# A two-layer graph network: another node order and packet size in the second edge layer, another placing of the sort's matmuls in the first

## What is computed

```python
def reference(x, src, dst, edge_type_8, L0_gnn_weight, L0_gnn_bias, L1_gnn_W_self, L1_gnn_W_neigh):
    edge_index = jnp.stack([src, dst])
    h = jnp.maximum(_layernorm(x, axis=-1), 0.0)
    x = x + _L0_gnn_ref(h, edge_index, edge_type_8, L0_gnn_weight, L0_gnn_bias)
    h = jnp.maximum(_layernorm(x, axis=-1), 0.0)
    x = x + _L1_gnn_ref(h, L1_gnn_W_self, L1_gnn_W_neigh, src, dst)
    return x
# L0: row, col = edge_index (so row = src, col = dst)
#     out = segment_sum((h[col] @ weight[edge_type]), row);  relu(out + bias)
# L1: h_self = feat @ W_self;  h_neigh = feat @ W_neigh
#     h_sparse = h_neigh with all but the 32 largest of each row set to 0
#     h_self + segment_sum(h_sparse[src], dst) / max(degree(dst), 1)
```

## Time and profile before

| | us |
|---|---|
| median of 3 runs | 3860.12 (3858.58 to 3865.2) |
| profiled execution, its own time | 3839.47 |
| span of the profile | 3837.8 |
| VectorE busy | 3257.8 (85%) |
| TensorE busy | 2697.9 (70%) |
| GpSimd busy | 2214.7 (58%) |
| ScalarE busy | 1896.3 (49%) |

### The profile page before, as it was taken

The page is one execution under the profiler, slowest core; times in us unless marked ns, Lnnn a source line. Parts: engine busy times, 40 slices in busy tenths (PEclk is TensorE's granted clock), DMA queues, the critical chain, the costliest instruction groups (busy, mean ns, idle before and its releaser), DMA issues.

```text
span 3837.8 us, 66966 instructions
## 1 busy us (share of the span) xinstructions
PE 2697.9 (70%) x10746; PEld 1702.6 (44%) x10747; DVE 3257.8 (85%) x14074; ACT 1896.3 (49%) x5805; POOL 2214.7 (58%) x1536
## 2 busy tenths in 40 slices
PE   2554767667788888886777777777777755767776
PEld 1222655555566666665333333333333324445554
DVE  8998778888888888885799999999999994555556
ACT  0000233333333333333577767777677756777776
POOL 0001886667777777777455555555555535565554
PEclk9998888888899999998888888888888888888888
DMA  9600466666555555555244444444444427777776
GB/s 349 231 0 29 76 116 146 147 146 143 103 101 100 102 100 100 101 101 105 106 161 159 153 153 158 161 157 157 153 157 161 159 106 234 227 245 236 240 231 201
DMA packets 307277, 576.89 MB, mean 150 GB/s; under 512 B 32005, under 2 KB 187944, under 8 KB 307214
## 3 DMA queue, kind: packets, MB, share of 16 engines
q1 hardware_dynamic: 211598, 419.86, 32.6%
q0 software_dynamic: 95616, 156.31, 20.9%
HBM read 317.16 MB, written 258.88 MB: 150 GB/s over the span
## 4 chain that ended last, share of the span: by engine, by line
DVE 38%; issue 32%; PE 15%; DMA 5%; POOL 3%; DVEq 3%; ACT 2%; ACTq 0%; POOLq 0%; another core or an unknown queue 0%; SPq 0%
DVE zone_c L1148 12%; PE banks L1516 7%; DVE best L1143 6%; DMA agg<-msg,sidx 4%; PE banks L1418 3%; DVE zone_c L1155 3%; DVE zone_c L1032 2%; DVE zone_c L1036 2%; DVE zone_c L1034 2%; DVE cross L932 2%; PE banks L1361 2%; PE banks L1429 2%; POOL rows_in L647 1%; DVE zone_c L1182 1%; DVE stats L878 1%
## 5 line engine op out<-in xcount | busy, mean ns | idle before, releaser
L1494 PE MATMUL banks<-w,hT 128*128 128x512 f32 x1568 | 836.3, 695 | 192.3 <-ACT hT L1282 192.3
L659 POOL DMA_INDIRECT agg<-msg,sidx x400 | 658.0, 1645 | 223.2 <-issue 114.3
L647 POOL DMA_INDIRECT rows_in<-in_x,gidx x400 | 436.1, 1090 | 480.5 <-DVE gidx L894 350.1
L1148 DVE MATCH_REPLACE8 zone_c<-best,zone_c 128x256 f32<-128x256 f32 x1568 | 623.1, 407 | 0.0
L1182 DVE SCALAR_TENSOR_TENSOR zone_c<-banks,rdeg,zone_c 128x256 f32 x784 | 379.3, 484 | 287.0 <-PE banks L1516 151.5
L1516 PE MATMUL banks<-w,zone_c 128*128 x1568 | 460.8, 452 | 228.5 <-issue 88.3
L1494 PEld LDWEIGHTS banks<-w,hT 128*128 128x128 f32 x1568 | 340.1, 223 | 632.5 <-issue 522.0
L1143 DVE MAX8 best<-zone_c 128x8 f32<-128x256 f32 x1568 | 547.5, 410 | 4.2
L703 POOL TENSOR_TENSOR zone_c<-msg,zone_c 128x1024 f32<-128x1024 f32 x98 | 232.7, 2374 | 512.3 <-ACT zone_c L1270 512.3
L718 POOL DMA_INDIRECT w<-hs,gidx x392 | 371.3, 947 | 263.0 <-issue 121.3
L1418 PE MATMUL banks<-w,hT 128*128 x1600 | 480.3, 428 | 19.0 <-issue 17.4
(11 more groups left out here) (224 smaller groups left out, 5057.8 us busy)
## 6 DMA issues: line engine op xcount, KB each, us to landing
out_rows<-zone_c SPq DMA_DIRECT2D x196, 512.0 KB, 2.6
agg<-bias SPq DMA_DIRECT2D x2, 25344.0 KB, 102.9
zone_c<-agg SPq DMA_DIRECT2D x98, 512.0 KB, 4.7
hs<-zone_c SPq DMA_DIRECT2D x98, 512.0 KB, 3.0
zone_c<-out_rows SPq DMA_DIRECT2D x98, 512.0 KB
rows_in<-in_x SPq DMA_DIRECT2D x97, 512.0 KB, 3.9
keyrow<-key_rows SPq DMA_DIRECT2D x100, 320.0 KB
zone_c<-bucket_rows SPq DMA_DIRECT2D x25, 512.0 KB
```

What stands on the lines that cost most here:

```text
L647: pool.indirect_dma_start(out=rows_in[p][:, j, :], out_offset=None, in_=x[:, :], in_offset=bass.IndirectOffsetOnAxis(ap=gidx[p][:, j:j + 1 ...
L659: pool.indirect_dma_start(out=agg[:, :], out_offset=bass.IndirectOffsetOnAxis(ap=sidx[p][:, j:j + 1], axis=0), in_=msg[p][:, j * D:(j + 1) ...
L1148: last = v.match_replace(work[:, j, :], best[:, j, :], (work if k else neigh[p])[:, j, :], NEG)
L1494: last = mm(bank[4 + j][:, :], hT[p][:, c, j * P:(j + 1) * P], w1[:, c, :], start=(c == 0), stop=(c == KC - 1))
```

## The change

Three things change.

1. **Nodes per bucket.** The bucket of node n is no longer n / 128 but (n / 512) * 4 + n mod 4, and its place in the bucket is (n / 4) mod 128. So one partition's rows of a group of four buckets are four neighbouring rows of DRAM, and the loads and stores of `y` become 4 KB runs. `bucket_row`, `bucket`, `low7` and `low16` are computed in another way, with as many VectorE instructions as before. The type sort still needs the true target, so the first *sort* body gets four more VectorE instructions of 128x512 that encode the new number (`encode`).
2. **Ranking.** `RC` goes from 16 to 14 and `RCHUNKS` from 25 to 28, so *rank* has 30 bodies and *rest* 2. The pad for tiles beyond 392 is gone.
3. **TensorE's order.** `hist_count`, `rank_choose` and `sort_place` have their waits at j = 2 and their matmuls in two halves, behind j = 2 and j = 3.

```diff
-        RC, RCHUNKS = 16, 25
+        RC, RCHUNKS = 14, 28
...
-                sp.dma_start(y[:, g * B:(g + 1) * B, :], out[bass.ds(k * BE, BE), :].rearrange("(j p) d -> p j d", p=P)
+                sp.dma_start(y[:, g * B:(g + 1) * B, :], out[bass.ds(k * BE, BE), :].rearrange("(p j) d -> p j d", j=B)
...
-                sp.dma_start(out[bass.ds(k * BE, BE), :].rearrange("(j p) d -> p j d", p=P), y[:, q * B:(q + 1) * B, :]
+                sp.dma_start(out[bass.ds(k * BE, BE), :].rearrange("(p j) d -> p j d", j=B), y[:, q * B:(q + 1) * B, :]
...
-            link(v.tensor_scalar(tmp_i[:, :], from0[:, :], 7, None, ALU.arith_shift_right))
-            link(v.tensor_copy(bucket[:, :], tmp_i[:, :]))
-            link(v.tensor_scalar(code16_i, from0[:, :], P - 1, None, ALU.bitwise_and))
-            link(v.tensor_copy(low7[:, :], code16_i))
-            link(v.tensor_scalar(tmp_i[:, :], tmp_i[:, :], LO - 1, None, ALU.bitwise_and))
-            link(v.tensor_copy(low16[:, :], tmp_i[:, :]))
             link(v.tensor_scalar(tmp_i[:, :], from0[:, :], 9, None, ALU.arith_shift_right))
             link(v.tensor_copy(high16[:, :], tmp_i[:, :]))
+            link(v.tensor_scalar(code16_i, from0[:, :], LO - 1, None, ALU.bitwise_and))
+            link(v.tensor_copy(low16[:, :], code16_i))
+            link(v.scalar_tensor_tensor(bucket[:, :], tmp_i[:, :], float(LO), code16_i, ALU.mult, ALU.add))
+            link(v.tensor_scalar(tmp_i[:, :], from0[:, :], 2, None, ALU.arith_shift_right))
+            link(v.tensor_scalar(tmp_i[:, :], tmp_i[:, :], P - 1, None, ALU.bitwise_and))
+            link(v.tensor_copy(low7[:, :], tmp_i[:, :]))
...
                         slots_of_positions()
+                        link(v.scalar_tensor_tensor(tab["type"][:, :], bucket[:, :], float(P), low7[:, :], ALU.mult,
+                                                    ALU.add))
+                        encode(tab["type"][:, :], DST_CODE)
...
+            def half(j, n):
+
+                return range((2 * j - B) * n // B, (2 * j - B + 2) * n // B)
...
             def sort_place(c, p, j):
-                if j == 0:
+                if j == B // 2:
                     pe.wait_ge(sort_hot, c + 1)
-                for t in range(j * CC // B, (j + 1) * CC // B):
+                for t in half(j, CC):
...
-                    if phase == "sort":
+                    if j >= B // 2 and phase == "sort":
                         sort_place(c, pc, j)
```

More of the change, by code:

```diff
@@ L622, in _ @@
             nc.gpsimd.memset(raw["dst"][:, last, :], N).then_inc(consts, 1)
-            nc.gpsimd.memset(starts_pad[:, :, :], 0.0)
             nc.gpsimd.memset(ident[:, :], 0.0)
@@ L779, in _ @@
                 link(v.tensor_copy(rawf[n][:, :, :], raw[n][:, :, :]))
-            for shift_by, rows16 in ((7, bucket_row), (9, high_row)):
-                link(v.tensor_scalar(raw["type"][:, :, :], raw["dst"][:, :, :], shift_by, None, ALU.arith_shift_right))
-                link(v.tensor_copy(rows16[:, :, :], raw["type"][:, :, :]))
+            link(v.tensor_scalar(raw["type"][:, :, :], raw["dst"][:, :, :], 9, None, ALU.arith_shift_right))
+            link(v.tensor_copy(high_row[:, :, :], raw["type"][:, :, :]))
+            link(v.tensor_scalar(raw["dst"][:, :, :], raw["dst"][:, :, :], LO - 1, None, ALU.bitwise_and))
+            link(v.scalar_tensor_tensor(bucket_row[:, :, :], raw["type"][:, :, :], float(LO), raw["dst"][:, :, :],
+                                        ALU.mult, ALU.add))
             v.memset(key0[:, SLOTS:COLS], float(N)).then_inc(rawf_done, 1)
@@ L786, in _, with encode @@
                 link(v.tensor_copy(tab[n][:, :], bank[k][:, :]))
+            def encode(number, code):
+                link(v.tensor_scalar(tmp_f[:, :], number, float(HALF), float(SIGN - HALF), ALU.is_ge, ALU.mult))
+                link(v.scalar_tensor_tensor(code16[:, :], number, float(CODE), tmp_f[:, :], ALU.add, ALU.add))
+                link(v.tensor_copy(field(code), code16[:, :].bitcast(F16)))
             for n, code in (("src", SRC_CODE), ("dst", DST_CODE)):
[L789 to L791 removed]
+                encode(tab[n][:, :], code)
             link(v.tensor_copy(from0[:, :], tab["dst"][:, :]))
[L793 to L798 removed]
             link(v.tensor_scalar(tmp_i[:, :], from0[:, :], 9, None, ALU.arith_shift_right))
             link(v.tensor_copy(high16[:, :], tmp_i[:, :]))
+            link(v.tensor_scalar(code16_i, from0[:, :], LO - 1, None, ALU.bitwise_and))
[4 more added lines that the diff above has]
+            link(v.tensor_copy(low7[:, :], tmp_i[:, :]))
             for r in range(R):
@@ L1373, in edge0_degree @@
                     last.then_inc(degrees0, 1)
+            def half(j, n):
+                return range((2 * j - B) * n // B, (2 * j - B + 2) * n // B)
             def hist_count(c, p, j):
-                if j == 0:
+                if j == B // 2:
                     pe.wait_ge(hist_hot, c + 1)
                     wait_from(pe, hist_out, c - 1, c, 2)
-                for t in range(j * HC // B, (j + 1) * HC // B):
+                for t in half(j, HC):
                     last = mm(bank[SORT + p][0:HI, t * LO:(t + 1) * LO], high_hot[p][:, t, :], low_hot[p][:, t, :],
@@ L1385, in rank_choose @@
             def rank_choose(c, p, j):
-                if j == 0:
+                if j == B // 2:
                     pe.wait_ge(rank_hot, c + 1)
                     wait_from(pe, rank_own, 4 * (c - 1), c, 2)
-                for t in range(j * RC // B, (j + 1) * RC // B):
-                    if isinstance(c, int) and c * RC + t >= TILES:
-                        of = starts_pad[0:HI, c * RC + t - TILES, :]
-                    else:
-                        of = starts16[0:HI, bass.ds(c * RC + t, 1), :].rearrange("p t l -> p (t l)")
+                for t in half(j, RC):
+                    of = starts16[0:HI, bass.ds(c * RC + t, 1), :].rearrange("p t l -> p (t l)")
                     last = mm(bank[SORT + p][:, t * 2 * LO:(t + 1) * 2 * LO], high_of[p][0:HI, t * P:(t + 1) * P], of,
@@ L1449, in edge0_body @@
                     edge0_degree(b, p, j)
-                    if phase == "hist" and c < HCHUNKS:
+                    if j >= B // 2 and phase == "hist" and c < HCHUNKS:
                         hist_count(c, pc, j)
-                    if phase == "rank" and inside(c, RCHUNKS):
+                    if j >= B // 2 and phase == "rank" and inside(c, RCHUNKS):
                         rank_choose(c, pc, j)
-                    if phase == "sort":
+                    if j >= B // 2 and phase == "sort":
                         sort_place(c, pc, j)
```

4 lines of the change are left out of this document (removed).

## The result

| | before | after |
|---|---|---|
| median | 3864.13 us (3858.58 to 3868.43, 7 runs) | 3845.33 us (3840.57 to 3852.68, 7 runs) |
| ratio | | 0.9951, 95% interval 0.9937 to 0.9964 |
| span of the profile | 3837.8 us | 3843.6 us |

The account below looks back on a forecast made before the run. VectorE with TensorE's late product bound sort; near-equal engines and DMA latency the second edge layer. Terms 0.5 - 2 - 8.7 + 2.5 - 26 - 9 = -42.7 took 3860.1 to 3817.4 us, range 3783 to 3850.

Parts of the forecast that it names:

- Term 4: Second edge layer: 4 KB transfers of y cut 0.47 us from each of 37 landing waits; half counted, -9 us.
- Term 2: Ranking: 14 tiles a group give 28 bodies of 14.65 us and three fewer of rest, -8.7 us.
- Term 1: Sort: TensorE's wait for one-hots moves behind product 2, so VectorE waits less for std, -26 us.
- term 3: In hist, the same matmul reordering, but GpSimd is the bound there, -2 us.
- Rival A: Sort: the stall only moves as TensorE's clock falls, bodies stay at 13.64 us, total 3843 us; 15%.
- the break-even: Ranking: a body of 14.96 us, at which the smaller groups neither gain nor lose.
- Rival D: Ranking: bodies do not shrink, the adds' latency holds them at 15.3 us, total 3837 us; 15%.
- the small ones: Four new VectorE instructions in the first sort body, +2.5 us, and changed instructions in the preparation, +0.5 us.
- Rival B: The second edge layer follows its DMA time, so all 46 us go, total 3780 us; 12%.
- E: Second edge layer: transfers of y stay at 1 KB runs, no gain there, total 3826 us; 2%.
- Rival C: Second edge layer: long packets of y hold gathers longer, 76 us over 37 waits, total 3902 us; 8%.
- The sentence that the prediction would be wrong altogether: Sign: the prediction fails if the second edge layer moves by more than 30 us either way.

Follow-up runs that it names:

- rc14_only: Only the ranking group size changed, 14 tiles in place of 16, against the kernel before; ratio 0.9993.
- late_only: Only TensorE's new matmul order, against the kernel before; ratio 0.9911, median 3827.8 us.
- late_rc14: TensorE's new order and 14 tiles a group, without the new node numbers and 4 KB transfers, against the kernel before; ratio 0.993, median 3834.5 us.
- late_y: TensorE's new order with the new node numbers and 4 KB transfers, 16 tiles a group, against the kernel before; ratio 0.9898.
- late_y_2: TensorE's new order with the new node numbers and 4 KB transfers, ranking as before, against the kernel before on chip D; ratio 0.9913.
- after_2: The full changed kernel once more, against the kernel before on chip D; ratio 0.9924.
- late_only_2: Only TensorE's new matmul order, repeated against the kernel before on chip D; ratio 0.991.
- y_quarter: The kernel before with only one of four buckets of y loaded and stored per group, against the kernel before; ratio 0.9799.
- after_again: The full changed kernel, unchanged, run again against the kernel before on chip B; ratio 0.9949, median 3841.3 us.
- y_half_rows: The kernel before with only two of four buckets of y loaded and stored per group, against the kernel before; ratio 1.006.
- y_half_cols: The kernel before with only 128 of 256 columns of y loaded and stored, against the kernel before; ratio 1.0045.

## Why the prediction was wrong in size, point by point

Two steps of the sum failed. Term 4 took 0.47 us off each of 37 waits for a landing, 9 us after halving, and got nothing: the sum of the packet times fell, the time for which the transfers of `y` last did not. Term 2 took a ranking body of 14.65 us, 8.7 us in all, where bodies measured 14.82 to 14.96 and the part gave 4 us at best. A cost that stood in no term, some 7 us in *sort*, came on top. Term 1 (with term 3) gave some 6 us more than forecast, which was luck; without it the result would have been further off.

**Term 1, TensorE's order: right, a little low.** Forecast -26 us, and -28 with term 3, which the same edit brings; measured -34 (chip B) and -33 (chip D, 3773.9 against 3807.3). In the traces *sort* fell by 28.5 us on chip B (750.4 in rc14_only, 721.9 in late_only), with `std` waits of 19.7 us against the 19 worked out, and the body is 13.12 us where 13.1 was read off. That GpSimd holds it there was argued and is not tested. The 4 us allowed for the low clock were not needed: the granted clock fell from 0.96 to 0.95 and the bodies shrank all the same. Rival A is refuted.

**Term 2, ranking: the body of 14.65 us failed.** A body shrank to 14.82 (after) and 14.87 to 14.96 elsewhere; 14.96 is the break-even that the prediction itself names. VectorE's busy time per body fell by 333.0 / 25 - 355.86 / 28 = 0.61 us, and the body by 0.52 in the profile of after. I had taken 0.69, more than VectorE's own saving, because earlier products were to help GpSimd's adds. The adds do land in time more often (40.5 to 19.7 us of waits), but they don't with earlier products alone (37.7 us in late_only, whose body stays at 15.3 us), and VectorE's wait for gathers rose from 20.3 to 25.4 us, GpSimd's for `msg` from 20.0 to 32.6. So about -4 us in the profile of after in place of -8.7, -2.7 by the ratio of rc14_only with an interval that reaches past zero, and a loss of 3 to 7 us on top of the late matmuls. Rival D, bodies that don't shrink, is half right.

**A term that was not there: +7 us in *sort*.** With all three parts the sort body is 13.26 to 13.29 in each of three traces; with the late matmuls and one other part (late_rc14, late_y, late_y_2) it is 13.13 to 13.16. The costliest sort one-hots on VectorE, late_y_2 first and after_2 behind:

```profile
L1038 DVE TENSOR_SCALAR zone_c<-iota_h,fields 128x128 f16<-128x128 f16 x383 | 131.0, 342 | 2.0
L1042 DVE TENSOR_SCALAR zone_c<-iota_h,fields 128x392 f16<-128x392 f16 x384 | 123.0, 320 | 0.0
```

```profile
L1036 DVE TENSOR_SCALAR zone_c<-iota_h,fields 128x128 f16<-128x128 f16 x385 | 127.6, 332 | 2.0
L1040 DVE TENSOR_SCALAR zone_c<-iota_h,fields 128x392 f16<-128x392 f16 x385 | 126.4, 328 | 0.0
```

One kind took 3.4 us more and the other 3.4 less, so the instructions' own times do not explain it. Yet VectorE is busy 671 to 673 us in the three traces with all parts against 665, and GpSimd 571 to 572 against 579 to 583. From start to start VectorE's body is 0.14 us longer in after_2 than in late_y_2, and half of that, 0.07 us, stands between two one-hots at one place near its beginning (0.24 to 0.31 us). That is where the gain of the 14 tiles goes, and more: after_2 is 0.11 points behind late_y_2. What sets it was not found.

**Term 3 and the small ones: right.** *hist* -2.6 (forecast -2). The stretch with the first sort body is 3.1 us longer (40.8 to 43.9, late_only_2 to late_y_2; forecast +2.5), the preparation 0.8 (381.4 to 382.2; +0.5), which is within its scatter: it ends at 381.0 to 381.9 us in traces of the old code, at 381.4 to 382.5 in those of the new.

**Term 4, the transfers: the step "taking 0.47 from each of 37", and with it "I count half", failed.** The DMA time fell by 36 us where 46 were forecast (45.6 engine-us per MB on chip D, 47.3% x 16 x 536 / 89.00, not 44.1), and of that none or 3 us reached the path on chip D, while on A the part cost 12.7 us. The step took 0.47 us off each wait for a landing, as if a pair of transfers would last that much less. On D it did not: SyncE's queue was moving for as long as before, a load still took 5.7 us, and the waits stayed at 90 us. That the traffic matters on such a chip is shown by y_quarter on C (0.9799); what the 4 KB runs saved was engine time inside an unchanged duration. Why the duration stayed was not tested. Where the waits for landings did fall (A, and after), the ring's wait took their place (on A landings 51.8 to 28.7 us, ring 80.4 to 121.5): TensorE frees the ring but runs at most eight steps (banks) ahead of VectorE, whose loop heads and pauses did not get shorter. I had priced VectorE by its busy time of 379 us and left out that `issue` and part of "PE banks" in its own row are idle time of its own. Rival B, the whole 46 us, is out, and so is E: the packets of `y` are 4 KB long. Rival C's 76 us supposed that a gather waits for a quarter of a pair with short packets and for all of it with long ones, which no run shows: a gather's last packet came 3.6 us after its issue with 1 KB packets on A and 3.5 us with 4 KB, and on D 3.6 us with either. The sentence that the prediction would be wrong altogether if this stage moved by 30 us names the right place: in the profiles it moved by 34. But most of that is the execution profiled before, whose 665.7 us is the shortest of all traces on such chips; unchanged code of that stage took 674.5, 684.7, 689.5 and 688.2, and the changed code 689.9 in after_again. That the sign pointed at the right stage was in part luck.

**The sum, read again on chip D:** -33.4 (late matmuls), +1.9 (second-layer part, late_only_2 to late_y_2), +3.4 (14 tiles), together -28.1, which is after_2. On B it is -35.7, +6.8 (the second-layer part, added last) and +6.7 (14 tiles), together -22.2; on the chip of the result the same kernel is 19 us faster. The steps of 2 to 7 us are near what such medians can tell. late_only (0.9911, 0.991) is the better kernel.

## What to carry to other kernels

Moving an engine's wait behind the work that others need was priced well from a body's timeline (26 us forecast, 28 measured in *sort*). An engine's floor in a loop is its busy time plus what each turn of the loop costs (in y_quarter 8.28 us and 2.9 a turn): look at the pattern of its idle time over the turns before calling it unsaturated. And the sum of packet times is not the time for which a transfer holds the others up (on D the sum fell from 324 to 288 us, and a load took 5.7 us before and after): read the time from issue to landing, and ask whether that shrinks. Small terms of such a stage are to be measured on more than one chip: here the worth of one part went from 0 to -12.7 us with the chip.

## What the hardware showed that I had not expected

- The chips of these runs differ in one stage only: the first layer takes 1403 to 1406 us on C and E alike (kernels with the old order of matmuls), and the second edge layer begins at 3168.9 us on C (y_quarter) and at 3168.8 on E (y_half_rows). That layer takes 624 to 629 us on C and D and 666 to 700 on the first, A and B, in kernels that move all of `y`. On the slower ones the sequencers of four engines show blanks of about 0.7 us in that stage, in front of instructions that wait for nothing; on C and D there are none in it.
- A loop's turn with its load of 32 registers cost VectorE 2.9 us in each of 48 turns of y_quarter (8.28 us of work), put down in the profile to TensorE; the load's own record is 2.3 us.
- 4 KB in place of 1 KB packets took 36 us off the DMA engines' summed time on D (324 to 288), and the queue was moving for 370 us as before; a 512 KB load still took 5.7 us.
- Less DMA traffic went with a slower kernel: 1.006 with half the transfers of `y` on E, where a quarter had given 0.9799 on C. Why is open.
- A packet of `y` took 29 ns at 512 B (y_half_cols), 52 at 1 KB (before) and 184 at 4 KB (late_y_2; 189 in after), means over the stage.
